# Second activation quantisation of an FFN kept in its hidden-major layout, inside a five-stage pipelined transformer kernel

## What is computed

```
h = silu(depthwise_conv1d(bit_linear(x, w1)))        # hidden 512
scale = 127 / max(max_over_hidden(|h|), 1e-5)        # one scale per token
hq = clip(round(h * scale), -128, 127) / scale
out = einsum('bsd,hd->bsh', hq, wq2)                 # 512 -> 128
```

## Time and profile before

| | |
|---|---|
| median of 3 runs | 1295.87 us (1292.59 to 1296.09) |
| the profiled execution | 1295.0 us, span 1293.1 us |
| TensorE matmuls / weight loads busy | 1155.8 us (89%) / 820.4 us (63%) |
| VectorE busy | 1064.0 us (82%) |
| ScalarE busy | 866.3 us (67%) |
| GpSimd busy | 693.4 us (54%) |
| mean granted TensorE clock | 0.957 of full speed |

### The profile page before, as it was taken

How to read it: one execution, slowest core, us unless ns; L and a number is a source line. 1 busy time by engine, 2 the same in 40 slices (tenths; PEclk the granted TensorE clock), 3 DMA queues, 4 the chain that set the end, 5 groups by cost and what they waited for, 6 DMA issues and landing times.

```text
span 1293.1 us, 27899 instructions
## 1 busy us (share of the span) xinstructions
PE 1155.8 (89%) x10338; PEld 820.4 (63%) x10338; DVE 1064.0 (82%) x2837; ACT 866.3 (67%) x1684; POOL 693.4 (54%) x827
## 2 busy tenths in 40 slices
PE   1567578999999999999999999999999998999998
PEld 1334345776767676776767676776767676667776
DVE  3667877889899889889899889889899888868653
ACT  0245456867767676867767676867767676866665
POOL 3212224556573837466573837566573837455765
PEclk9566779999999999999999999999999999999999
DMA  6000001001010101001010101001010101000000
GB/s 195 20 12 10 12 25 29 17 8 39 10 43 9 37 17 37 17 8 39 10 43 9 37 17 37 17 11 36 10 43 9 37 1 37 16 9 16 10 9 9
DMA packets 63846, 32.69 MB, mean 25 GB/s; under 512 B 29280, under 2 KB 63072, under 8 KB 63328
## 3 DMA queue, kind: packets, MB, share of 16 engines
q1 hardware_dynamic: 61696, 26.83, 8.3%
q10 hardware_dynamic: 2016, 4.08, 0.9%
HBM read 24.73 MB, written 4.19 MB: 22 GB/s over the span
## 4 chain that ended last, share of the span: by engine, by line
PE 63%; DVE 25%; ACT 6%; issue 3%; POOL 1%; SPq 1%; DMA 1%; POOLq 0%; DVEq 0%; ACTq 0%
PE py L699 12%; PE pa L544 5%; PE pa L532 4%; PE pa L508 3%; DVE q_st L1075 3%; PE pg L689 3%; DVE moe L1196 3%; PE pu L689 3%; PE pg L691 3%; PE pg L690 3%; PE pu L691 3%; PE pu L690 3%; DVE acc L1209 2%; ACT probs L758 2%; ACT st_t L754 2%
## 5 line engine op out<-in xcount | busy, mean ns | idle before, releaser
L897 POOL TENSOR_TENSOR moe<-moe 128x512 f32<-128x512 f32 x256 | 329.2, 1290 | 375.3 <-DVE moe L1196 191.5
L699 PEld LDWEIGHTS py<-wd_s,moe 128*128 128x128 f32 x1856 | 234.8, 192 | 19.5 <-issue 1.5
L699 PE MATMUL py<-wd_s,moe 128*128 128x128 f32 x1856 | 244.3, 276 | 0.1
L1075 DVE TENSOR_REDUCE q_st<-pa 128x4 f16<-128x480 f32 x256 | 168.0, 656 | 42.7 <-PE pa L508 40.4
L820 ACT ACTIVATE tg<-pg 128x512 f32<-128x512 f32 x232 | 139.7, 602 | 85.1 <-PE pg L691 84.3
L1196 DVE SCALAR_TENSOR_TENSOR moe<-tg,pg 128x512 f32<-128x512 f32 x232 | 157.7, 680 | 15.0 <-ACT tg L820 12.6
L758 ACT ACTIVATE probs<-pa 120x512 f32<-120x512 f32 x256 | 138.9, 597 | 37.5 <-PE pa L532 35.8
L834 ACT ACTIVATE moe<-pu 128x512 f32<-128x512 f32 x232 | 138.9, 599 | 12.5 <-PE pu L691 8.7
L508 PE MATMUL pa<-kbd,qkht 128*128 128x480 f16 x256 | 100.3, 392 | 30.4 <-DVE q_st L1075 23.2
L689 PE MATMUL pg<-x4h,wg_h 128*128 128x512 f16 x232 | 89.0, 384 | 18.1 <-DVE moe L1196 14.8
L858 POOL TENSOR_SCALAR xn<-x,lnm,lnr 128x128 f32<-128x128 f32 x192 | 87.7, 469 | 5.2
(11 more groups left out here) (200 smaller groups left out, 2708.8 us busy)
## 6 DMA issues: line engine op xcount, KB each, us to landing
xin<-in_x SPq DMA_DIRECT2D x16, 256.0 KB, 2.8
xres<-in_x SPq DMA_DIRECT2D x16, 256.0 KB, 3.0
kbd<-qkht SPq DMA_DIRECT2D x256, 7.5 KB
out_x<-acc SPq DMA_DIRECT2D x16, 256.0 KB, 4.1
ctxt_a<-in_ctx_t SPq DMA_DIRECT2D x16, 240.0 KB, 2.7
ctxt_b<-in_ctx_t SPq DMA_DIRECT2D x16, 240.0 KB, 3.5
ctxn_b<-in_ctx SPq DMA_DIRECT2D x16, 240.0 KB, 4.2
wd_s<-in_wd ACTq DMA_DIRECT2D x1, 1024.0 KB, 9.0
```

Of the source, the lines that this page charges most:

```text
L699: mm = pe.matmul(moe_y(g, e)[:, j, :], hu[:, u % 3, j * S:(j + 1) * S], wd_s[:, u, :], start=(half == 0 and j == 0), stop=(half == 1), ski ...
L897: pool.tensor_tensor(hu[:, u % 3, :], gw[:, u % 3, :], us[:, u % 3, :], ALU.mult)\
L1075: dve.tensor_reduce(q_st[:, t, 4 * c:4 * c + 4, 3 * HD], pa[:, BM, 0:4 * SC].rearrange("p (h k) -> p h k", h=4), AX.X, ALU.max, negate=Tru ...
```

## The change

- The hidden tile is no longer turned. VectorE takes for each partition and token the maximum of |h2| over the four blocks (`hmx`, one reduction of 128x2048 to 128x512); TensorE turns that small tile (four 128x128 pieces), and VectorE reduces each to the four maxima of a partition (`am2`, 128x4).
- The scales, now with a token on each partition, are written on the diagonal of four 128x128 matrices (`dg`), and one fp32 matmul of `ones` with `dg` (`sbc`) gives every partition the scale of every token. ScalarE copies it back over `dg`.
- GpSimd multiplies `h2` by it, block by block (`round`), ScalarE adds MAGIC in place and subtracts it into `hi_t`, one block behind.
- `hmx` and `dg` lie in the two halves of `hr`, which is free now.
- The values matmuls of a sequence are one step of 16 products instead of two steps of 8 (the step ("values", t, 0) is still in the list and issues nothing).
- All strings of `TURNS` but those of the first and last kind are new; the step list of b has seven steps for the old eight.

```diff
--- before.py
+++ after.py
@@ -43,7 +43,7 @@
 MAGIC = 12582912.0
 RSQRT_SEED = 1597463007.0
 WSCALE = 64.0
-LINKS_N, LINKS_A, LINKS_B, LINKS_D = 13, 4, 23, 7
+LINKS_N, LINKS_A, LINKS_B, LINKS_D = 13, 4, 14, 7
 S0, S1, BM, BO, PB = range(5)
 BANK = {"xn1t": S0, "q": S1, "k": S0, "v": S1, "qkht": S0, "d": S1}
 
@@ -65,54 +65,54 @@
...
-        "nab": "bbaaaaaabaaaabbnaaaabaaabbbabaabnaabbbaabaabanbabaaaabaabnaababanaanbabna",
+        "nab": "abaaaaabaabaaaabaaabbbbaaaabbnbaabaaanaababbbbaaaabanabaaaabnnanabnbabaa",
...
@@ -187,7 +187,8 @@
         am2, sc2, inv2 = (sb(n, [128, GB]) for n in ("am2", "sc2", "inv2"))
         hr = sb("hr", [128, 2, HID])
         w1_f, w2_f = hr[:, 0, :], hr[:, 1, :].rearrange("p (k d) -> p k d", k=KB)
-        hi_t = sb("hi_t", [128, GB, KB, S], BF16)
+        hmx, dg = hr[:, 0, :], hr[:, 1, :]
+        hi_t = sb("hi_t", [128, KB, T], BF16)
         x2, x2b = sb("x2", [128, GB, D]), sb("x2b", [128, GB, D])
         xn3t, bft = sb("xn3t", [128, T]), sb("bft", [128, T])
         nmax1 = sb("nmax1", [128, GB])
@@ -273,9 +274,10 @@
         fc1_ps = signal("fc1_ps", KB)
         mid_done, cv_done = signal("mid_done", KB), signal("cv_done", KB)
         th_done, h2_done = signal("th_done", KB), signal("h2_done", KB)
-        h2t_ps, sc2_done = signal("h2t_ps", GB), signal("sc2_done", GB)
-        hr_done = signal("hr_done", GB)
-        hit_ps, hit_done = signal("hit_ps", GB), signal("hit_done", GB)
+        hmx_done, hmx_ps = signal("hmx_done"), signal("hmx_ps")
+        am2_done, dg_done, sbc_ps = signal("am2_done"), signal("dg_done"), signal("sbc_ps")
+        sbc_done, y2_done = signal("sbc_done"), signal("y2_done", KB)
+        r2_done, hi_done = signal("r2_done", KB), signal("hi_done", KB)
         fc2_ps, x2_done = signal("fc2_ps"), signal("x2_done")
         x2b_done = signal("x2b_done")
         ln_ready = signal("ln_ready", 2)
@@ -336,7 +338,7 @@
         for k in range(KB + 1):
             steps = [("taps", k - 1), ("fc1", k), ("silu", k - 1)]
             b_steps += [step for step in steps if 0 <= step[1] < KB]
-        b_steps += [(name, t) for t in range(GB) for name in ("h2t", "hit")] + ["fc2"]
+        b_steps += ["hmx", "am2", "sbc"] + [("round", k) for k in range(KB)] + ["fc2"]
         d_steps = ["ln3", "xn3t", "bf", "s1", "p1n", "p1t", "oc", "fused", "ln4", "xn4t", "gate"]
         c_steps = []
         for u in range(NU):
@@ -533,19 +535,17 @@
                                            st_t[r, NQ * S + n * SC:NQ * S + (n + 1) * SC],
                                            st_t[r, n * S:(n + 1) * S], start=True, stop=True)
                     mm.then_inc(s_ps.sem, 1)
-                elif name == "values":
-                    if c == 0:
-                        if t == 0:
-                            pe.wait_ge(v_done.sem, v_done.at(g))
-                        take(BO, o_done, g, t + 1)
-                    for i in (2 * c, 2 * c + 1):
+                elif name == "values" and c == 1:
+                    if t == 0:
+                        pe.wait_ge(v_done.sem, v_done.at(g))
+                    take(BO, o_done, g, t + 1)
+                    for i in range(HQ):
                         pe.wait_ge(p_done.sem, p_done.at(g, 4 * t + i + 1))
                         for n in range(NQ):
                             mm = pe.matmul(pa[32 * n:32 * n + HD + 1, BO, i * S:(i + 1) * S],
                                            v_st[0:SC, t, HQ * n + i, :], probs[0:SC, i, n, :],
                                            start=True, stop=True)
-                    if c == 1:
-                        mm.then_inc(o_ps.sem, 1)
+                    mm.then_inc(o_ps.sem, 1)
                 elif name == "turn":
                     take(BO, on_done, g, t + 1)
                     for i in range(HQ):
@@ -584,25 +584,22 @@
                     pe.matmul(pb[:, :], w1_i[:, t * 128:(t + 1) * 128], xh[:, :], start=True, stop=False)
                     pe.matmul(pb[:, :], w1_i[:, t * 128:(t + 1) * 128], xl[:, :], start=False, stop=True)\
                       .then_inc(fc1_ps.sem, 1)
-                elif name == "h2t":
-                    if t == 0:
-                        pe.wait_ge(h2_done.sem, h2_done.at(g, KB))
-                    take(PB, hr_done, g, t + 1)
-                    for k in range(KB):
-                        mm = pe.transpose(pb[:, k * 128:(k + 1) * 128], h2[:, k, t * S:(t + 1) * S], id_f[:, :])
-                    mm.then_inc(h2t_ps.sem, 1)
-                elif name == "hit":
-                    pe.wait_ge(hr_done.sem, hr_done.at(g, t + 1))
-                    take(PB, hit_done, g, t + 1)
-                    for k in range(KB):
-                        mm = pe.transpose(pb[:, k * S:(k + 1) * S], hr[:, t % 2, k * 128:(k + 1) * 128], id_f[:, :])
-                    mm.then_inc(hit_ps.sem, 1)
+                elif name == "am2":
+                    pe.wait_ge(hmx_done.sem, hmx_done.at(g))
+                    take(PB, am2_done, g)
+                    for j in range(GB):
+                        mm = pe.transpose(pb[:, j * 128:(j + 1) * 128], hmx[:, j * S:(j + 1) * S], id_f[:, :])
+                    mm.then_inc(hmx_ps.sem, 1)
+                elif name == "sbc":
+                    pe.wait_ge(dg_done.sem, dg_done.at(g))
+                    take(PB, sbc_done, g)
+                    pe.matmul(pb[:, :], ones[:, :], dg, start=True, stop=True).then_inc(sbc_ps.sem, 1)
                 elif name == "fc2":
-                    pe.wait_ge(hit_done.sem, hit_done.at(g, GB))
+                    pe.wait_ge(hi_done.sem, hi_done.at(g, KB))
                     take(PB, x2_done, g)
                     for j in range(GB):
                         for k in range(KB):
-                            mm = pe.matmul(pb[:, j * D:(j + 1) * D], hi_t[:, j, k, :], w2_i[:, k, :],
+                            mm = pe.matmul(pb[:, j * D:(j + 1) * D], hi_t[:, k, j * S:(j + 1) * S], w2_i[:, k, :],
                                            start=(k == 0), stop=(k == KB - 1))
                     mm.then_inc(fc2_ps.sem, 1)
 
@@ -777,14 +774,17 @@
                 elif name == "taps":
                     act.wait_ge(cv_done.sem, cv_done.at(g, t + 1))
                     act.activation(th[:, t % 2, :], cv[:, t % 2, :, :], ACT.Tanh, scale=0.5).then_inc(th_done.sem, 1)
-                elif name == "h2t":
-                    act.wait_ge(sc2_done.sem, sc2_done.at(g, t + 1))
-                    act.activation(hr[:, t % 2, :], pb[:, :], ACT.Identity, bias=magic[:, 0:1],
-                                   scale=sc2[:, t:t + 1]).then_inc(hr_done.sem, 1)
-                elif name == "hit":
-                    act.wait_ge(hit_ps.sem, hit_ps.at(g, t + 1))
-                    act.activation(hi_t[:, t, :, :], pb[:, :], ACT.Identity, bias=unmagic[:, 0:1])\
-                       .then_inc(hit_done.sem, 1)
+                elif name == "sbc":
+                    act.wait_ge(sbc_ps.sem, sbc_ps.at(g))
+                    act.activation(dg, pb[:, :], ACT.Copy).then_inc(sbc_done.sem, 1)
+                elif name == "round" or name == "fc2":
+                    if name == "round":
+                        act.wait_ge(y2_done.sem, y2_done.at(g, t + 1))
+                        act.activation(h2[:, t, :], h2[:, t, :], ACT.Identity, bias=magic[:, 0:1]).then_inc(r2_done.sem, 1)
+                    last = t - 1 if name == "round" else KB - 1
+                    if last >= 0:
+                        act.wait_ge(r2_done.sem, r2_done.at(g, last + 1))
+                        act.activation(hi_t[:, last, :], h2[:, last, :], ACT.Identity, bias=unmagic[:, 0:1])                           .then_inc(hi_done.sem, 1)
 
             def do_d(step, g):
                 name, pd = step, bank("d")
@@ -915,6 +915,10 @@
                 if name == "ln2":
                     pool.wait_ge(ln2_ready.sem, ln2_ready.at(g))
                     normalise(pow_b, pow_b.at(g, 2), 1, x1, xn2).then_inc(xn2_done.sem, 1)
+                elif name == "round":
+                    if t == 0:
+                        pool.wait_ge(sbc_done.sem, sbc_done.at(g))
+                    pool.tensor_tensor(h2[:, t, :], h2[:, t, :], dg, ALU.mult).then_inc(y2_done.sem, 1)
 
             def do_d(step, g):
                 if step == "ln3":
@@ -1124,16 +1128,29 @@
 
                     dve.wait_ge(cv_done.sem, cv_done.at(g, t + 1))
                     dve.wait_ge(th_done.sem, th_done.at(g, t + 1))
+                    if later(g):
+                        dve.wait_ge(hi_done.sem, hi_done.at(g - 1, t + 1))
                     dve.scalar_tensor_tensor(out=h2[:, t, :], in0=th[:, t % 2, :], scalar=1.0,
                                              in1=cv[:, t % 2, :, :].rearrange("p t s -> p (t s)"),
                                              op0=ALU.add, op1=ALU.mult).then_inc(h2_done.sem, 1)
-                elif name == "h2t":
-                    dve.wait_ge(h2t_ps.sem, h2t_ps.at(g, t + 1))
```

(23 more changed lines are left out.)

70 lines of the change are left out of this document (35 added, 35 removed).

## The result

| | before | after |
|---|---|---|
| median | 1295.28 us (1292.59 to 1296.09) | 1345.28 us (1342.63 to 1346.81) |
| profiled execution, span | 1293.1 us | 1345.0 us |
| granted TensorE clock, mean | 0.957 | 0.939 |

(The median before is over four runs: the three that stand above, and one more.) The change makes the kernel **slower by 50 us**, a ratio of 1.0388 with a 95% interval of 1.0364 to 1.0411. The prediction had 1276.6 us and a range of 1254 to 1306. The result lies outside both, on the other side.

A forecast was written before the change was run, and what follows sets the result against it. Full bodies alternate between TensorE and VectorE stretches; TensorE alone binds the drain, latency the fill. 1295.0 - 18 (full bodies) - 4.3 (drain) + 3 (fill) = 1275.7, plus 0.9 to the median: 1276.6 us; overall range 1254 to 1306.

The forecast's parts named there:

- The price of the reduction: VectorE's added reduction over four blocks: between 2.28 and 4.4 us, taken as 2.28, the row of equal size.
- VectorE's term: VectorE's work for each group: 4.72 us of maxima removed, 4.3 us added, 0.4 us less.
- Contention at zero: GpSimd and VectorE locking each other: 0.8 us a body against up to 0.95 back, taken as zero (-1.7 to +3).
- The starved instruction: Rival, 0.19: a GpSimd run without gaps holds VectorE's q product (L1065), 3 us a body, 1313 us.
- Stride: Rival, 0.05: the strided reduction costs two cycles an element, VectorE 1.7 us more a body and binding, 1314.6 us.
- The weights of the sum: In full bodies, TensorE's saving counts at 0.63 and VectorE's at 0.25, their chain shares: 1.5 us less a body.
- TensorE: TensorE's work for each group: eight transpose sets removed, one set and the product with ones added, 2.15 us less.
- Drain: Two draining bodies with stage b, bound by TensorE: 2 x 2.15 = 4.3 us gained.
- the cover: GpSimd's added products fit ahead of hidden products of units 11 and 12, the latter with a few microseconds to spare.
- Fill: While the pipeline fills: 3 us lost, all from the values step.
- Values step: Merged values on TensorE: nothing in a full body; 0.5 to 1.0 us lost for each of four filling sequences, 3 us.
- GpSimd and ScalarE: GpSimd's four added products, 5.1 us, hidden; ScalarE 5.9 us removed, 5.6 added with passes at 0.63, so nothing.

The follow-up runs named there:

- e12: e2 (third layer norm statistics moved ahead of the quantisation on VectorE) without GpSimd's four products of the round step; 1305.17 us, ratio 1.0078 to the kernel before.
- e6: Changed kernel with both repairs: reduction over neighbouring elements (e1) and third layer norm statistics ahead of the quantisation on VectorE (e2); 1285.17 us, ratio 0.9912 to before.
- e8: e6 without GpSimd's four products of the round step, so the values rounded are not scaled; 1282.93 us, ratio 0.9890 to before.
- e7: Changed kernel with the hidden tile as two planes of interleaved blocks, the right maxima, plus e2's moved step; 1288.46 us, ratio 0.9932 to before.
- e3: Kernel before with only the values product merged into one step, in the old orders; 1298.87 us, ratio 1.0020.
- e10: e7 with the values product again in two halves; 1304.74 us, ratio 1.0072 to before.
- e1: Changed kernel with its reduction reading the same 2048 elements side by side, so over other groups of maxima; 1315.78 us, ratio 1.0145 to before.
- e5: Changed kernel with the reduction's element distance set by group, 1 to 512 elements; one execution, 1336.5 us, only its reductions used.
- e11: Changed kernel without GpSimd's four products of the round step, values rounded unscaled; 1329.89 us, ratio 1.0269 to before.
- e2: Changed kernel with the third layer norm statistics moved ahead of the quantisation on VectorE in full bodies; 1320.88 us, ratio 1.0182 to before.
- e9: e1 with the full bodies in the orders of the kernel before, GpSimd's products behind units 10 to 13; 1425.67 us, ratio 1.0993 to before.

## Why the prediction was wrong

- **The price of the reduction** was the first step that failed. "I take 2.28, the row of equal size": it measured 3.74, inside the bounds (2.28 and 4.4) but nearer to the far end. The row of equal size had neither the distance nor anything that spoke for its being free, and a rule against it was in the text. It got 0.05 as a rival; an added operation with no row of its form in the trace, on an engine at 65 of 72 us, deserved the middle of its bounds. With 3.7 instead of 2.28 VectorE's term turns from 0.4 us less into 1 us more.
- **Contention at zero** was the second. The step set 0.8 us for the added products, by GpSimd's share of a body, against up to 0.95 given back, and took zero. The give-back came: the three products of the q/k norm got 1.0 us a body cheaper, and the one that stayed locked (L1061, 1.77 us) costs 0.1 us more than before. In e12 the lock of the added products on it was worth 1.1 us a body; before, an expert sum had held the same product as long. But the large item, 3.6 us a body on `silu`, has nothing to do with the share. It came from one step on VectorE, `ln3` behind `quant`, which let GpSimd run dry and then catch up without gaps. I followed the queue of the added products and did not follow who waits for the steps that changed places around them. The net of 2.6 us is inside the step's own bounds (-1.7 and +3).
- **The starved instruction**: the rival had the mechanism and the price (2.8 us and 0.2 behind it; measured 3.60 less 0.68 = 2.9 on the first `silu`, and 0.7 on the second). It named the wrong train and the wrong victim. L1065, "over 2 us shows the starving rival", was at 0.68, and yet bodies carried this cost.
- **Rivals as exclusive cases** was the third failed step. Stride and starvation were given 0.05 and 0.19, each alone, on 1314.6 and 1313. They occurred together. 1276.6 + 38.0 + 36.4 = 1351 us, 6 us from the result. That it comes so close is partly luck: the stride's share was priced at 2.1 us for 1.46 measured, and the 1.0 us that the q/k norm gave back is not in it. They are about different instructions and nothing made them exclude each other; a range that took in their sum would have held the time.
- **The weights of the sum.** 0.63 and 0.25, the shares of the chain of waits, hold for small changes only. When VectorE has 3.4 us more in a body with 7 us of room, it does not cost a quarter of that: it took over the chain (51%), and the body grew by 3.7.
- **TensorE**: 2.15 us less for a group in starts; busy fell by 1.4 to 1.8 us. The direction was right, and the forecast of 71 us for a body was near e6's 71.64. What was predicted for the change came true only once its two side effects were gone.
- **Drain**: 4.3 us gained was predicted, 3.0 us were lost. The last body with stage a did gain 1.6 us. In the next one TensorE waits for GpSimd (2.64 us, once): an expert's hidden product stands there behind three of the added products, the cover that the prediction called the first thing to go. The changed kernel's drain, and the kernel before at the same seam:

```profile
1201.30:1252.00 50.70, 46.43 (x290) 33.02 (x290) 41.74 (x106) 30.15 (x65) 33.72 (x40) 0.97 0.06 16
1252.00:1264.00 12.00, 8.91 (x61) 7.19 (x61) 6.93 (x17) 7.86 (x16) 8.79 (x8) 0.72 0.00 1
```

```profile
1203.00:1214.00 11.00, 10.82 (x91) 7.58 (x89) 8.63 (x26) 7.81 (x17) 7.23 (x7) 1.00 0.08 24
```

  TensorE idles for 3 of 12 us, at a granted clock of 0.72, where it was busy for 10.8 of 11. Without GpSimd's products the drain is 2.9 us shorter (e8 against e6). An order of that body that repairs it was not tried.
- **Fill**: it lost 4.2 us where 3 were predicted for the values step. Much of it stands beside the clock: in the two bodies ahead of the first full one it was 0.68 and 0.68 in the changed kernel, 0.75 and 0.81 before. That it is the values step is not shown: e6 and e7 have the same merged step and the same strings there, and with 211.7 and 210.1 us no loss in the fill.
- **Values step**: 3 us predicted, 2.4 measured in the old orders (e3). "In a full body nothing" held there, and was wrong in the new orders, where the merged step saves at least 0.6 us a body (e10).
- **GpSimd and ScalarE**: 5.1 us of products measured 5.3 (L921, 1355 ns) and hid in full bodies (e8). Eight passes were priced at 0.63 and took 0.72 (below), which ScalarE's idle time hid.

In sum: the two repairs give back 60 us where 50 were lost, and what is left, e6 against before, is a gain of 12 us, where the forecast had 19. e6 takes maxima over other values than the change does; e7, which takes the right ones, has 8.5 us of it. One thing stays open: what decides in which bodies the clock dips. Among the full bodies behind the first it does in four of the changed kernel, seven of e1, four of e10, five of e5, one of e11, and in none of e2, e6, e7, e8 and e12; in e9 it does in every one. Outside e9 a stop of TensorE stands beside it each time, 2.18 us at VectorE's row maximum in the changed kernel, e1, e5 and e11, 1.34 us ahead of a scores step in e10. But the same stops are in bodies of these kernels without a dip, and nothing was run on them alone.

## What to carry to other kernels

Before moving a layout change onto VectorE, look at the address pattern of each new operand: an fp32 reduction that takes its elements 16 bytes or more apart ran 1.6 times as long as one that takes two of a 16-byte line in a row, and interleaving pairs was enough to get it back. When an order is written anew, check for each engine-to-engine step that changed places who runs dry because of it, since here it was a train without gaps on GpSimd that held VectorE's instructions with two SBUF operands, not GpSimd's total load. And add up rivals that touch different instructions; they are not alternatives.

## What the hardware showed that was not expected

- The step between a distance of 8 and of 16 bytes, and its flatness up to 2 KB (e5); that a jump behind every second element is free (e7).
- A VectorE instruction that begins inside a GpSimd train can lose three GpSimd operations in a row (3.60 us in after), not one. It need not: with the same train and the same start to 0.01 us, `silu` took 3.61 us in ten full bodies of e1 and 1.15 in two. A start 0.06 us behind or 0.14 us ahead of GpSimd's made 1.77 or 0.69 us (e2, e6). The Trainium skill (SBUF — State Buffer, Who interferes with whom) says that the issue order, not the shape of the operation, decides who blocks; on this pair the trace agrees.
- A ScalarE pass with a per-partition bias tile takes longer than one without. From SBUF, `h<-h,magic` has 725 ns and the activation without bias tile 632:

```profile
L783 ACT ACTIVATE h<-h,magic 128x512 f32<-128x512 f32 x64 | 46.3, 725 | 1.4 <-POOL h L921 1.4
...
L776 ACT ACTIVATE th<-cv 128x512 f32<-128x512 f32 x64 | 40.4, 632 | 35.9 <-DVE cv L1125 34.6
```

  Out of PSUM it was 690 against 597, the same 93 ns, and 780 with a scale tile as well. The row I priced the rounding passes by had no bias tile.
